# A graph layer with gathered rows: GpSimd's two waits per chunk replaced by three, on other events

## The reference

```
h   = max(layernorm(x), 0)
he  = (h[src] + edge_attr) @ W                    # per edge, 2 heads x 64
s   = leaky_relu(<he, attn_l> + er[dst])          # er = <h @ W, attn_r> per node
p   = exp(s - segment_max(s, dst)[dst]);  alpha = p / segment_sum(p, dst)[dst]
ft  = segment_sum(he * alpha, dst).mean(heads)
out = x + relu(batchnorm(ft))
```

## Time and profile before

| | |
|---|---|
| median of three executions | 2416.4 us |
| profiled execution | 2423.31 us |
| its span | 2421.6 us |
| DVE busy | 1572.2 us (65%) |
| POOL busy | 1484.8 us (61%), of it 1414.7 us in 1498 gathers |
| PE busy | 765.5 us (32%) |
| ACT busy | 231.1 us (10%) |
| POOL's idle time that PE's sums ended | 380.0 us in 47 waits |

### The profile page before, as it was taken

The page is one execution under the profiler, slowest core; times in us unless marked ns, Lnnn a source line. Parts: engine busy times, 40 slices in busy tenths (PEclk is TensorE's granted clock), DMA queues, the critical chain, the costliest instruction groups (busy, mean ns, idle before and its releaser), DMA issues.

```text
span 2421.6 us, 17156 instructions
## 1 busy us (share of the span) xinstructions
PE 765.5 (32%) x4684; PEld 580.3 (24%) x4684; DVE 1572.2 (65%) x3611; ACT 231.1 (10%) x435; POOL 1484.8 (61%) x1579
## 2 busy tenths in 40 slices
PE   2323333232323333232323223232323333232325
PEld 2312222221212222121222222121222222122215
DVE  5758866765675566567657656765666567567556
ACT  2410000000000000000000000000000000000001
POOL 6756465666666566656656665666666566656640
PEclk9966555565555565555556555555655555655556
DMA  6322222222222222222222222222222122222124
GB/s 170 80 49 75 69 50 48 77 51 49 75 52 50 47 77 51 50 63 62 51 48 77 51 50 50 75 51 49 75 51 50 48 78 51 50 69 57 23 65 121
DMA packets 71352, 150.47 MB, mean 62 GB/s; under 512 B 28637, under 2 KB 31544, under 8 KB 64664
## 3 DMA queue, kind: packets, MB, share of 16 engines
q0 software_dynamic: 50208, 53.02, 12.9%
q1 hardware_dynamic: 19930, 92.57, 11.2%
q10 hardware_dynamic: 1112, 3.73, 0.6%
HBM read 141.17 MB, written 6.60 MB: 61 GB/s over the span
## 4 chain that ended last, share of the span: by engine, by line
DVE 55%; another core or an unknown queue 20%; issue 19%; PE 2%; SPq 1%; DVEq 1%; DMA 1%; ACT 1%; POOL 0%; ACTq 0%
DVE prods L1089 9%; DVE acc L1426 6%; DVE bond_el L1091 5%; DVE scaled L1398 4%; DVE work L1110 4%; DVE onehot L1241 2%; DVE ohT_i L1247 2%; DVE pen L1237 2%; DVE lanes L1346 1%; DVE lanes L1347 1%; SPq L521 1%; DVE p_r L1372 1%; DVE lanes L1373 1%; DVE p_r L1227 1%
## 5 line engine op out<-in xcount | busy, mean ns | idle before, releaser
L631 POOL DMA_INDIRECT work<-h_tab,srcI x1498 | 1414.7, 944 | 852.5 <-issue 440.1
L972 PE MATMUL po<-scaled,work 128*65 128x64 f32 x3104 | 396.6, 304 | 926.3 <-issue 922.4
L972 PEld LDWEIGHTS po<-scaled,work 128*65 128x65 f32 x3104 | 358.4, 219 | 962.2 <-issue 961.1
L1426 DVE TENSOR_TENSOR acc<-acc,po 65x64 f32 x776 | 168.6, 217 | 186.4 <-remote 157.6
L719 ACT ACTIVATE pt<-work 128x512 f32<-128x512 f32 x196 | 117.5, 600 | 1640.7 <-DVE work L1110 1356.4
L1089 DVE TENSOR_TENSOR prods<-pt,wb 128x1024 f32<-128x1024 f32 x188 | 229.1, 1219 | 28.9 <-issue 28.6
L1091 DVE TENSOR_REDUCE bond_el<-prods 128x16 f32<-128x1024 f32 x188 | 229.4, 1220 | 9.5 <-DVE prods L1089 1.9
L917 PE MATMUL p_s<-ohT_i,er_st 128*32 128x256 f32 x392 | 149.4, 550 | 7.0 <-DVE er_st L1249 7.0
L1237 DVE TENSOR_SCALAR pen<-pen 32x257 f32<-32x257 f32 x49 | 15.4, 315 | 202.3 <-remote 201.1
L1110 DVE TENSOR_TENSOR work<-work,pt 128x512 f32<-128x512 f32 x196 | 132.4, 676 | 0.7 <-ACT pt L719 0.5
L925 PE MATMUL p_s<-ident,elh 128*32 128x128 f32 x196 | 51.4, 417 | 209.6 <-DVE elh L1104 159.0
(11 more groups left out here) (197 smaller groups left out, 982.3 us busy)
## 6 DMA issues: line engine op xcount, KB each, us to landing
work<-in_ea_t SPq DMA_DIRECT2D x49, 1024.0 KB
ohT_i<-in_dst_n SPq DMA_DIRECT2D x49, 512.0 KB
work<-h_tab,srcI POOLq DMA_INDIRECT x1498
h_tab<-acc SPq DMA_DIRECT2D x1, 2887.5 KB
work<-in_x SPq DMA_DIRECT2D x1, 2800.0 KB
out<-work SPq DMA_DIRECT2D x5, 448.0 KB
acc<-in_x ACTq DMA_DIRECT2D x3, 672.0 KB
drow_i<-in_dst_r SPq DMA_DIRECT2D x49, 32.2 KB
```

The source lines that it names most:

```text
L631: pool.indirect_dma_start(out=row, out_offset=None, in_=x if c < RAW else h_tab, in_offset=bass.IndirectOffsetOnAxis(ap=srcI[:, c, j, g:g ...
L972: m = mm(bank[0:F1, w0:w0 + H * WIN], edge[c % 2][:, j, g, :], scaled[:, j * CG + g, :, :].rearrange("p h w -> p (h w)"), start=(j == 0), ...
L1426: added = v.tensor_tensor(at, at, bank[0:F1, w0:w0 + H * WIN].rearrange("p (h w) -> p h w", h=H), ALU.add)
```

## The change

Chunks 6 to 47 get three waits in place of two. Before, gather 1 of chunk c waited for the sums of chunk c-2 and gather 17 for the turned p of chunk c-1. Now gather 5 waits for the scores of chunk c-1, gather 12 for its turned p, and gather 21 for its sums. Chunk 5 and the last chunk, 48, keep their waits as they were. No other engine's instructions change.

```diff
             def keep_step_late(c, at):
 
-                last = c == NCH - 1
-                if at == 1:
-                    pool.wait_ge(sums_made, 2 * (c - 1))
-                elif at == (13 if last else 17):
-                    pool.wait_ge(p_turned, c - (c == LEAD or last))
-                elif last and at == 22:
+                if c == LEAD or c == NCH - 1:
+                    if at == 1:
+                        pool.wait_ge(sums_made, 2 * (c - 1))
+                    elif at == (17 if c == LEAD else 13):
+                        pool.wait_ge(p_turned, c - 1)
+                    elif c == NCH - 1 and at == 22:
+                        pool.wait_ge(sums_made, 2 * c)
+                    return
+                if at == 5:
+                    pool.wait_ge(scores_made, c)
+                elif at == 12:
+                    pool.wait_ge(p_turned, c)
+                elif at == 21:
                     pool.wait_ge(sums_made, 2 * c)
```

## The result

| | kernel before | changed kernel |
|---|---|---|
| median of five executions each | 2416.4 us (2410.13 to 2418.70) | 2429.1 us (2428.26 to 2435.51) |
| ratio of the means | 1 | 1.0067, 95% interval 1.0046 to 1.0087 |
| span of the profiled execution | 2421.6 us | 2433.8 us |
| POOL busy / idle before its gathers | 1484.8 / 852.5 us | 1484.6 / 864.9 us |

The changed kernel is 0.5% slower by the medians and 0.7% by the means. The spans differ by 12.2 us, the idle time of POOL by 12.4 us: POOL's work is the same and all of the difference is waiting.

What follows compares the result with a forecast made beforehand. Bound: a run of 32 gathers without a break, not DVE or PE. Start -9, 40 chunks 0, end +10 gave +1 us: span 2422.6, 2424.3 with 1.7 around it, less 6.9 for the profiled execution: 2417 us, range 2396 to 2450.

Steps and rivals of the forecast that it cites:

- The bound: Each chunk: 32 unbroken gathers (39.6 us), others released 5.3 us after the last, sums done 1.9 us later; period 47.35 us.
- The wait at 5 is free: Chunks 6 to 45: scores ready at T + 17.4, POOL arrives at T + 20.5, so no cost.
- The wait at 12 is free, with 2.7 us to spare: Chunks 6 to 45: p turned at T + 26.6, POOL there at T + 29.3, so no cost.
- forecast case: Whole kernel: two new waits passed, the third stops POOL 7.8 us as before; 2417 us, range 2404 to 2434, chance 0.60.
- the 0.3 us: Sign in the chunk period: a shift from 47.4 us by more than this would prove the forecast wrong.
- the crawl reaches the scores: Rival: DVE slows from its scans on, wait at 12 stops POOL; +3.3 us for 40 chunks, +132 us, 2549; chance 0.12.
- The start, -9: Chunk 5's sums end at 361.7 instead of 371.3, less half a us at the wait at 12; bounds -11 and -4.
- The end, +6 +3 +1: Chunk 47 beside 33 gathers +6, chunk 46's row loads +3, chunk 47's target load +1; +10 us, bounds -3 and +24.
- Fuller store: Rival: PE gets 50 sum matmuls through before its stall, not 41; -20 us likely, 2397; chance 0.19.
- Gathers under DVE's long products: Gathers moved there would stretch according to the Trainium skill; forecast says they average 944 ns regardless and adds nothing.
- the end costs in full: Rival: 33 gathers before chunk 47's sums move them by 15 us, with chunk 46's 8; 2432; chance 0.09.

Runs made afterwards that it cites:

- free executions: Executions, of unchanged or changed kernels, in which no engine runs slowly while POOL gathers; the kernel before takes 2022 to 2026 us there, against 2416 to 2431 otherwise.
- the repeat: The changed kernel itself run again, no further edit: 2428.27 us beside 2418.55 for the kernel before, ratio 1.0045.
- the two kernels that would have shown it: Changed kernel with chunk 47's old waits (ratio within 0.9993 to 1.0016); kernel before with new waits in chunks 6 to 10 and other edits (2023.13 us, 1.0002).
- the kernel with the part count: Kernel before, but POOL's gather 1 (chunks 5 to 47) waits for 48 of the 64 sum matmuls: ratio 0.9996, run again 0.9989.
- the one with four stretches: Changed kernel, no wait at 12 and/or wait at 21 for 48 of 64 matmuls in some chunks, chunk 48 held: 2448.47 us, 1.0081 to kernel before.
- its four variants: Changed kernel without wait 12; with wait 21 alone; with chunk 47's old waits; with chunk 48 held for chunk 47's scores: ratios 1.0007, 1.0004, 1.0002, 1.0004.

## Why the prediction was right and where it failed

The time, 2429.1 us, lies in the range (2396 to 2450) and 12 us above the number. The range is wide, and part of the nearness is luck: 5.2 us that stood at the start before the first changed wait (below) hid as much of the cost that the forecast left out. Step by step:

- **The bound** was read rightly for these executions: a run of 32 gathers, a release behind POOL's stop, 41 matmuls before the stall. The changed kernel shows 41 to 44 again in 37 of 40 chunks. In the sum of a period two small errors cancel: POOL starts at T + 0.27 and not 0.55, and from its last gather to the end of the sums it is 7.4 us and not 7.2. The free executions have no such stall; no row of the prediction could tell that.
- **The wait at 5 is free**: right, scores at T + 16.6, POOL at T + 20.2.
- **The wait at 12 is free, with 2.7 us to spare**: this is the step that failed. It carried p over at its old distance from the scores, 9.2 us. It took 13.3 us in chunk 23, because the scans now lie 18 to 28 us behind POOL's restart and the crawl sets in 23.4 us behind it. The kernel before shows that point too: in chunk 40 DVE first stood (before L1313) 24.5 us after T39. The pause at 12 adds 1.6 us on average (0.8 us or more in 31 of 40 chunks), and the time from POOL's last gather to the end of the sums falls from 7.4 to 6.1 us: +1.6 - 1.4 is +0.2 by this count, +0.23 by the period, 9.3 us in 40 chunks. In the repeat it is +1.1 - 0.9. A pause for p in most chunks is what the prediction itself named as the sign that its forecast case is wrong; the period moved by less than the 0.3 us that it named beside it. The rival "the crawl reaches the scores" named this mechanism and priced it at 3.3 us a chunk, fourteen times too much. It put p at T + 36, and the median came at 29.9. Even in chunk 18, with p at T + 34.5 and a pause of 6.1 us, the sums ended 2.0 us behind POOL's last gather and not 3.5 us, and the chunk took 48.0 us: what the pause costs is mostly given back behind the run.
- **The start, -9**: T5 came 14.0 us earlier. Of it 5.2 us stood already at T3 (271.4 against 276.6), ahead of the first changed wait; chunk 2's sums took 5.9 us where they had taken 12.0, and 6.5 in the repeat. No changed wait can act there, but all three profiles of kernels with the new waits have T3 at 271.2 to 272.1, and of the kernel before there is one crawling profile, so it is open whether the 5.2 us are chance. If they are, the change's own part is -8.8. The lead of T3 was gone at T4 (324.1 in both), as forecast: four more gathers stood before the sums of chunk 4.
- **The end, +6 +3 +1**: 16.9 in all. Chunk 46 cost 0.55 and not 3. The target load cost 5.6 us and not 1 (L1254 at T46 + 8.6 in place of 3.0; 6.6 in the repeat). The scans of chunk 47, priced at 6, cost nothing; the additions of chunk 46 and the products among them cost 10. The size came near, the place was wrong: I asked what the gathers would do to the scans and not what they would do to all that stands between T46 and them. DVE stood 4.67 us at L1325, the first instruction behind the branch (4.62 in the kernel before), and 4.5 to 5.0 us in the free executions too, where nothing crawls, so this pause is the branch's own. Two fetches of instructions, of 8 KB each, fall into it in all 14 traces: the first starts 1.5 to 2.0 us after DVE has stopped, the second ends within 0.2 us of its going on. The Trainium skill ("Runtime: NRT & Kernel Launch", Instruction fetch mechanics) says that a taken branch makes the engine wait for a fetch if its target lies outside the two pages that it holds; the trace agrees, though no row tells which engine's fetches these are. That the scans behind it then cost nothing is no proof for it: POOL had stopped at 2350.5, before they began.
- **Fuller store**: not seen in the form named; PE had 41 matmuls in chunk 23 although it had idled longer before them. Where PE did get 56 to 59 through, in three chunks, a long pause of POOL's at gather 12 had come before.
- **Gathers under DVE's long products**: not stretched, as forecast. In the kernel before 368 gathers that overlap L1089 or L1398 take 944 ns on average, and the others 945 ns.
- **The rival "the end costs in full"** adds 14 us and not 15 (15 + 8 in place of 6 + 3).

By the count of gathers start and end look like the same thing. The wait for the sums stands 12 gathers earlier, 15 us, so POOL runs ahead by less from chunk 6 on, and 33 gathers instead of 21 are left behind T46. Gained 8.8, paid 16.4. That one is the price of the other is argued from the counts and was not shown; the two kernels that would have shown it met free executions.

## What to carry to other kernels

A wait that is "passed with 2.7 us to spare" is only passed if the work before it keeps its pace: when a change moves work to another phase of a neighbour's burst, price each of its instructions by the rows of that phase, not by its old distances. When a throttle is moved earlier by n transfers, look for the n transfers at the end; here they lay there beside 16.4 us of loss. And before explaining a stall that no event ends, see whether other executions have it at all: here a sixth of the time hung on it, and every variant tied without it.

## What the runs showed that was not expected

**The bound of the kernel before is not always there.** In the free executions of the kernel with the part count, whose extra waits stand at the same gathers as before:

```profile
L634 POOL DMA_INDIRECT work<-h_tab,srcI x1498 | 1417.7, 946 | 459.0 <-issue 455.8 <-PE po L975 2.6 <-DVE work L1115 0.6
L975 PE MATMUL po<-scaled,work 128*65 128x64 f32 x3104 | 295.6, 283 | 217.5 <-issue 214.4 <-DVE scaled L1403 2.5 <-DVE scaled L1397 0.6
```

The gathers take the same 946 ns and are issued at the same distance; what is missing are the pauses. The 64 sum matmuls of a chunk run in one piece while POOL gathers:

```profile
1031.14 0.42 PE L957 MATMUL p_m<-ident,pT 32*128 32x32 f32 x2 [1.95 <-ACT pT L801]
1036.22 6.65 PE L975 MATMUL po<-scaled,work 128*65 128x64 f32 x64 [4.66 <-issue]
```

So the gathers and their transfers alone do not make the others crawl.

**What differs with it is the record.** The view of DMA issues names the time to landing in free executions:

```profile
work<-in_ea_t SPq DMA_DIRECT2D x49, 1024.0 KB, 7.4
ohT_i<-in_dst_n SPq DMA_DIRECT2D x49, 512.0 KB, 3.8
work<-h_tab,srcI POOLq DMA_INDIRECT x1498, 2.5
```

In crawling ones it has none for these three, and most of the semaphore records that such a time needs are missing. Counted in the traces: 33,053 and 33,101 records of raised semaphores in two free executions; 7,223 in the kernel before, 9,285 and 9,109 in the changed kernel, 8,186 in the one with four stretches. In chunk 23 of the kernel before, from 1206 to 1218, they come one each 0.7 us on average, the step of the crawl (the additions above go at 1.40 us, two such steps), while at 1226.65, 2.1 us behind POOL's restart, 13 come within 0.3 us. Fetches of instructions don't fit it: the trace holds 39 of 16 KB and 63 or 64 of 8 KB in all, in both kinds. A likely reading is that the crawl is the engines waiting for a recorder of events that POOL's gathers keep busy, and the store that empties is its buffer. I could not test this, as no execution comes without the record; it stays open, and with it whether the 0.7% would be seen in a kernel that nobody profiles. What is shown is that the change costs 0.5 to 0.7% where the crawl is. Where it isn't, the changed kernel itself was not run; its four variants, one of them with all of its waits, cost nothing that could be told.
